# Start of an AdaLN/FFN kernel: up's second quarter on SP's queue, squares of group three behind x's first half, up's rest in two

## The reference

```python
w = weights[conditions]                       # (128, 32, 32) out of (200, 32, 32)
hs = einsum('bct,bcd->bdt', x, w)             # x: (128, 32, 256)
top = top_k(hs @ gate_w, 2)                   # 8 experts, only the two values are used
h = square(relu(hs @ up_w))                   # 256 -> 1024
y = h @ down_w + (hs @ expert_w) * top.sum()  # 1024 -> 256
out = x + (y - mean(y)) / sqrt(var(y) + 1e-5) * gamma + beta
```

## Time and profile before

| | us |
|---|---|
| median of 3 runs | 229.46 (229.46 to 229.64) |
| the profiled execution | 229.29 |
| its span, first to last instruction | 227.6 |
| TensorE busy | 220.9 (97% of the span) |
| VectorE busy | 160.9 (71%) |
| GpSimd busy | 131.4 (58%) |
| ScalarE busy | 106.4 (47%) |
| mean granted TensorE clock | 0.998 of full speed |

### The profile page before, as it was taken

One profiled execution on the slowest core, in us unless ns is written; L12 is line 12 of the kernel. 1 busy time (PEld: TensorE's weight loads), 2 busy tenths in 40 slices (PEclk: granted clock), 3 DMA queues, 4 the chain that ended last, 5 costly groups with the idle time before them and its releaser, 6 DMA issues.

```text
span 227.6 us, 3998 instructions
## 1 busy us (share of the span) xinstructions
PE 220.9 (97%) x1260; PEld 191.4 (84%) x1260; DVE 160.9 (71%) x352; ACT 106.4 (47%) x187; POOL 131.4 (58%) x131
## 2 busy tenths in 40 slices
PE   7899999999999999999999999999999999999992
PEld 2798888888888889888889888888888888888892
DVE  6587965777667777667667766577766766777885
ACT  3379865444555345534545444544454444444000
POOL 3758795665545763656455764366555575557411
PEclk9999999999999999999999999999999999999999
DMA  3877123030603010000200002000020002000031
GB/s 98 231 213 230 50 59 103 10 98 7 187 10 98 9 66 30 0 0 3 92 0 0 3 0 95 3 0 0 0 95 1 0 0 68 28 0 0 10 108 69
DMA packets 17177, 11.81 MB, mean 52 GB/s; under 512 B 6660, under 2 KB 16900, under 8 KB 17156
## 3 DMA queue, kind: packets, MB, share of 16 engines
q1 hardware_dynamic: 15460, 10.43, 15.1%
q10 hardware_dynamic: 1280, 1.07, 1.4%
q0 software_dynamic: 416, 0.05, 0.2%
HBM read 7.35 MB, written 4.19 MB: 51 GB/s over the span
## 4 chain that ended last, share of the span: by engine, by line
PE 94%; DMA 1%; issue 1%; DVE 1%; ACTq 1%; POOLq 0%; POOL 0%; ACT 0%; DVEq 0%
PE up_ps L337 39%; PE down_ps L431 25%; PE down_ps L433 13%; PE hid_ps L303 5%; PE moe_ps L449 3%; PE moe_ps L448 3%; PE moe_ps L447 3%; DMA wd<-in_L_cond_weights_dram 1%; PE down_ps L303 1%; ACTq L513 1%; DMA cond_row<-in_itok_B_dram 1%; POOLq L46 0%; POOL rstd L697 0%; DVE result L615 0%; DVE stats L588 0%
## 5 line engine op out<-in xcount | busy, mean ns | idle before, releaser
L682 POOL TENSOR_TENSOR sq_lo<-square,sq_hi 128x512 fp32r<-128x512 f32 x64 | 84.4, 1322 | 77.0 <-DVE square L553 77.0
L431 PE MATMUL down_ps<-down_hl,sq_hi 128*128 128x512 f32 x248 | 88.8, 393 | 0.0
L553 DVE SCALAR_TENSOR_TENSOR square<-up_ps,relu 128x512 f32<-128x512 f32 x64 | 44.0, 687 | 37.3 <-ACT relu L491 28.2
L433 PE MATMUL down_ps<-down_hl,sq_lo 128*128 128x256 f32 x248 | 69.6, 280 | 0.0
L431 PEld LDWEIGHTS down_ps<-down_hl,sq_hi 128*128 128x128 f32 x248 | 46.5, 188 | 10.8 <-issue 0.3
L491 ACT ACTIVATE relu<-up_ps 128x512 f32<-128x512 f32 x64 | 38.2, 596 | 35.8 <-PE up_ps L337 35.7
L337 PE MATMUL up_ps<-hid_hi,up_hi 128*128 128x512 f32 (+1 forms) x136 | 52.8, 391 | 0.3 <-ACT hid_hi L476 0.3
L337 PE MATMUL up_ps<-hid_hi,up_lo 128*128 128x512 f32 (+1 forms) x136 | 51.1, 379 | 0.0
L433 PEld LDWEIGHTS down_ps<-down_hl,sq_lo 128*128 128x128 f32 x248 | 46.7, 188 | 2.4
L493 ACT ACTIVATE sq_hi<-relu 128x512 fp32r<-128x512 f32 x64 | 40.6, 634 | 2.0
L337 PE MATMUL up_ps<-hid_lo,up_hi 128*128 128x512 f32 (+1 forms) x136 | 40.6, 381 | 0.0
(11 more groups left out here) (62 smaller groups left out, 193.3 us busy)
## 6 DMA issues: line engine op xcount, KB each, us to landing
x_sb<-in_x_dram SPq DMA_DIRECT2D x7, 512.0 KB, 4.2
out_dram<-result SPq DMA_DIRECT2D x7, 512.0 KB, 3.0
wd<-in_L_cond_weights_dram SPq DMA_DIRECT2D x111, 4.0 KB, 1.5
x_sb<-in_L_ffn_down_w_dram SPq DMA_DIRECT2D x2, 512.0 KB, 4.7
x_sb<-in_x_dram ACTq DMA_DIRECT2D x2, 256.0 KB, 2.9
result<-in_L_ffn_up_w_dram ACTq DMA_DIRECT2D x2, 256.0 KB, 2.9
result<-in_L_ffn_up_w_dram SPq DMA_DIRECT2D x1, 512.0 KB, 4.7
out_dram<-result SPq DMA_DIRECT2D x4, 128.0 KB, 1.7
```

Of the source, the lines that this page charges most:

```text
L431: pe.matmul(dst[:, :], a_hi, down_hl[:, c, :, :].rearrange("p s t -> p (s t)"), start=(c == 0), stop=False)
L433: mm = pe.matmul(dst[:, T:2 * T], a_lo, down_hl[:, c, 0, :], start=False, stop=(c == CH - 1))
L553: dve.scalar_tensor_tensor(square[:, c % 2, :], up_ps[c % UPB][:, :], 0.0, relu[:, c % 2, :], ALU.max, ALU.mult).then_inc(square_done, 1)
L682: pool.tensor_tensor(sq_lo[:, j % 2, c, :], square[:, c % 2, :], sq_hi[:, j % 2, c, :].bitcast(f32), ALU.subtract).then_inc(sq_lo_done, 1)
```

## The change

Four things move, all of them in the first 20 us of the program. The number and shape of the matmuls stay the same.

- Up's second quarter is issued by SP directly behind the first part of the condition row; before, ScalarE issued it behind the rounding of the first quarter. The rest of the condition row, before on SP, is the first thing that GpSimd issues.
- Of the squares of groups three and four, GpSimd issues 8 to 11 (the whole of group three) and waits for x's first half before it does; SP issues 12 to 15 (the whole of group four). TensorE waits for each group by a semaphore of its own, and the products of the second half run group by group.
- Up's second half is still one load (`UP_LOADS`), but it is rounded and split in two parts (`UP_SPLITS` has four now): chunks 4 and 5 where the whole was before, chunks 6 and 7 behind the experts' subtraction and behind the second square.
- ScalarE's queue has one load less, so x's second half is issued right behind the rounding.

```diff
-UP_SPLITS = [slice(0, 2), slice(2, 4), slice(4, CH)]
+UP_LOADS = [slice(0, 2), slice(2, 4), slice(4, CH)]
+UP_SPLITS = [slice(0, 2), slice(2, 4), slice(4, 6), slice(6, CH)]
...
-BY_SP, BY_ACT, BY_POOL, BY_SP_LATER = (0, 2, 4, 6), (1, 3, 5, 7), (8, 9, 10, 11, 12), (13, 14, 15)
+BY_SP, BY_ACT, BY_POOL, BY_SP_LATER = (0, 2, 4, 6), (1, 3, 5, 7), (8, 9, 10, 11), (12, 13, 14, 15)
...
-            cond_flat = cond.rearrange("(o b) -> o b", o=1)
             sp.dma_start(cond_row[:, 0:TILES * Q], cond_flat[:, 0:TILES * Q]).then_inc(cond_first_landed, 16)
-            sp.dma_start(cond_row[:, TILES * Q:ROWS_B], cond_flat[:, TILES * Q:ROWS_B]).then_inc(cond_later_landed, 16)
+            load_up(sp, 1)
             sp.wait_ge(cond_first_landed, 16)
...
             for b in BY_SP_LATER:
-                sp.dma_start(square_of(b), weights_of(values[b])).then_inc(wd_later_landed[0], 16)
+                sp.dma_start(square_of(b), weights_of(values[b])).then_inc(wd_first_landed[b // Q], 16)
...
             def conditioning_first(half):
                 pe.wait_ge(x_first_landed[half], 16)
-                if half == 0:
-                    pe.wait_ge(wd_first_landed[0], 16 * Q)
-                    condition(0, 0, 0)
-                    condition(0, 1, 0)
-                    pe.wait_ge(wd_first_landed[1], 16 * Q)
-                    condition(0, 0, 1).then_inc(hid_done, 1)
-                    condition(0, 1, 1).then_inc(hid_done, 1)
-                else:
-                    pe.wait_ge(wd_later_landed[0], 16 * len(BY_SP_LATER))
-                    pe.wait_ge(wd_later_landed[1], 16 * len(BY_POOL))
-                    for k in range(K):
-                        condition(0, k, 2)
-                        condition(0, k, 3).then_inc(hid_done, 1)
+                g = 2 * half
+                pe.wait_ge(wd_first_landed[g], 16 * Q)
+                condition(0, 0, g)
+                condition(0, 1, g)
+                pe.wait_ge(wd_first_landed[g + 1], 16 * Q)
+                condition(0, 0, g + 1).then_inc(hid_done, 1)
+                condition(0, 1, g + 1).then_inc(hid_done, 1)
...
             split_up(0)
-            load_up(act, 1)
             load_x_first(act, 1)
...
+            def round_up(part):
+                dve.tensor_copy(up_hi[:, :, split_cols(part)], up_raw[:, :, split_cols(part)]).then_inc(up_hi_ready, 1)
...
             dve.wait_ge(up_landed[2], 16)
-            dve.tensor_copy(up_hi[:, :, split_cols(2)], up_raw[:, :, split_cols(2)]).then_inc(up_hi_ready, 1)
+            round_up(2)
             split_up(2)
...
                             .then_inc(eg_lo_ready, 1)
+                        round_up(3)
+                    if j == 0 and c == 1:
+                        split_up(3)
...
+            pool.dma_start(cond_row[:, TILES * Q:ROWS_B], cond_flat[:, TILES * Q:ROWS_B]).then_inc(cond_later_landed, 16)
             pool.memset(minus_half[:, :], -0.5).then_inc(consts_ready, 1)
...
             pool.wait_ge(wd_zeroed[0], 1)
+
+            pool.wait_ge(x_first_landed[0], 16)
             for b in BY_POOL:
-                pool.dma_start(square_of(b), weights_of(values[b])).then_inc(wd_later_landed[1], 16)
+                pool.dma_start(square_of(b), weights_of(values[b])).then_inc(wd_first_landed[b // Q], 16)
```

More of the change, by code:

```diff
@@ L109, in adaln_ffn @@
         x_landed = {j: sem(f"x_landed{j}") for j in range(1, BLOCKS)}
-        up_landed = [sem(f"up_landed{n}") for n in range(len(UP_SPLITS))]
+        up_landed = [sem(f"up_landed{n}") for n in range(len(UP_LOADS))]
         down_landed = [sem(f"down_landed{n}") for n in range(DOWN_LOADS)]
@@ L113, in adaln_ffn @@
         cond_first_landed, cond_later_landed = map(sem, ("cond_first_landed", "cond_later_landed"))
-        wd_first_landed = [sem(f"wd_first_landed_group{g}") for g in range(TILES // 2)]
-        wd_later_landed = [sem("wd_later_landed_sp"), sem("wd_later_landed_pool")]
+        wd_first_landed = [sem(f"wd_first_landed_group{g}") for g in range(TILES)]
         wd_second_landed = [sem("wd_second_landed_sp"), sem("wd_second_landed_pool")]
@@ L220, in weights_of, with load_up @@
             return cond_w[bass.ds(row, 1), :, :].rearrange("s c d -> (s c) d")
-        def load_up(queue, part):
-            cols = split_cols(part)
-            queue.dma_start(up_raw[:, :, cols], up_rows[:, :, cols]).then_inc(up_landed[part], 16)
+        cond_flat = cond.rearrange("(o b) -> o b", o=1)
+        def load_up(queue, load):
+            cols = slice(P * UP_LOADS[load].start, P * UP_LOADS[load].stop)
+            queue.dma_start(up_raw[:, :, cols], up_rows[:, :, cols]).then_inc(up_landed[load], 16)
         def load_x_first(queue, half):
```

## The result

The changed kernel takes 230.51 us (median of 6 runs, 230.46 to 230.62) against 229.55 for the kernel before on the same chip (229.39 to 229.78). The ratio is 1.0041, 95% interval 1.0028 to 1.0054: 0.94 us slower. The forecast was 229.6 with a range up to 230.2, so the time lies outside it, on the slower side; "no change" had been given 0.66. Of the executions named further down, one of e10's twelve (277.2 us, at a granted clock of 0.757) is left out of its ratio.

A forecast was written before the change was run, and what follows sets the result against it. TensorE, with 94% of the chain of waits, was taken as the bound. From 229.29 us, +0.2 for the start and -0.07 for the split gave 229.42; with 0.17 to the median, 229.6, range 229.2 to 230.2.

The forecast's parts named there:

- part 5: Up's rest in two parts on VectorE: first chunk's square about 0.4 earlier, -0.07 us; second parts and later squares cost 0.
- The 0.07 behind chunk 3: TensorE's lateness at chunk 4, 14.48 instead of 14.41, waiting for the first square's bank; forecast to go, -0.07 us.
- Part 1: Up's second quarter on SP at the start: squares land later behind the larger bulk, +0.2 us, range -0.3 to +0.75.
- parts 1 to 4: Start +0.2 us; ScalarE's queue, groups three and four with GpSimd's wait, and SP's later issues each 0.
- Part 3: Groups three and four: GpSimd's squares wait for x's first half, starting about 4.5, landing 9.1, wanted 9.73; cost 0.
- Part 4: All of SP's later issues move by 0.5, second block's squares wanted at 16.69; cost 0, range 0 to +0.45 us.
- A: Crowded start: first two groups' squares pile up behind 768 KB, landing 0.5 to 0.75 later; 230.0 us; chance 0.18.
- B: Second block's squares: SP's 0.5 delay reaches TensorE at 16.69, +0.45, 229.9 us; chance 0.10.
- C: Freer start: with GpSimd silent, group two lands up to 0.3 earlier; 229.1 us; chance 0.10.
- D: GpSimd's issue is held: its squares miss 9.73 by 0.5 or more; 229.9 to 230.1 us; chance 0.04.
- the 0.26 for "slower": Chance of exceeding 229.92 us: A 0.15, half of B 0.05, D and a tail of the forecast 0.06.

The follow-up runs named there:

- e10: Kernel before with up's rest in two parts and the experts' rounding and subtraction ahead of the first relu and square; ratio 1.0012, 0.28 us over before.
- e2: Kernel before with up's rest rounded and split in two parts, loads unchanged; ratio 1.0037, 0.85 us over before.
- e1: Changed kernel with up's rest rounded and split whole, as before; ratio 1.0001 against the kernel before (0.9992 to 1.0009).
- e4: Changed kernel with GpSimd's first square rest waiting for the experts' subtraction; ratio 1.0027, 0.62 us over the kernel before.
- e6: Changed kernel with the experts' rounding and subtraction ahead of the first relu and square; ratio 0.9995 against the kernel before.
- e5: Changed kernel with both operations on up's last quarter moved behind the third square; ratio 1.0053, 1.2 us over the kernel before.
- e8: Kernel before with only GpSimd's squares held until x's first half has landed; ratio 1.0035, 0.8 us over before.
- e7: e3 with GpSimd's squares also held until x's first half has landed; ratio 1.0019, 0.44 us over the kernel before.
- e3: Kernel before with up's second quarter issued by SP, the row's rest behind it, GpSimd's squares not held; ratio 1.0039, 0.9 us over before.
- e9: e6 with squares 6 and 7 of the second group issued by GpSimd without the hold; ratio 1.0047, 1.1 us over the kernel before.
- e11: e10 with squares 6 and 7 issued by GpSimd and 11 to 15 by SP; ratio 1.0099, 2.3 us over the kernel before.

## Why the prediction was wrong, point by point

- **The step that failed is part 5**: "Cost 0" for the second parts, with "the squares of chunks 1 and 2 come some 0.4 later at most, with four banks ahead". The second square came 1.57 later, and the cost was 0.85 (e2) to 0.92 (after against e1). I had looked for the consumer of the squares among the banks `up_ps`, where there was indeed room. The consumer with little cover was another: GpSimd's chain of rests, and behind it the scale of the experts in VectorE's queue, with 0.39 to TensorE. It had its rows in the trace (GpSimd without a break from 14.48 to 21.62) and I did not follow them.
- The same part missed **what an earlier operation triggers**. "The square can start about 0.4 earlier" was right, but its only user in the next microsecond was GpSimd, which then worked beside the experts' subtraction. That the subtraction doubles by it (0.71 to 1.48) is shown by e4. That the order of this turn decides is shown by e6, where both added operations stay and the loss goes; behind a flipped turn the rounding makes the lateness larger (e5). The 0.07 behind chunk 3 did go away: chunk 4 follows at 0.24 after the last pair instead of 0.31.
- **Part 1 (start, +0.2)** was right in kind and in size as far as the runs can tell: 0.2 to 0.4 by e1, e5 and e6. The changed kernel's own profile has +0.47, but TensorE's slow warm-up bounds it there. ScalarE's squares landed in 2.2 to 2.6 instead of 1.7 to 2.0:

```profile
DMA to landing us min/median/max: 2.2/2.4/2.6
```

  The bulk was through between 4.5 and 5.0 (the slices have 378 and then 99 GB/s), as worked out. But the three loads did not end together, and x's first half was not later, as the prediction had it: it took 2.7 (2.8 in the kernel before) and landed at about 3.7, up's second quarter at 4.5 (3.2 after its issue) and up's first quarter at 5.3 (3.8, where before none of ScalarE's loads took more than 3.1). In the total the delay of the start was nearly given back: e1, which is parts 1 to 4 alone, is level with before within 0.2, where the parts' sum had been +0.2.
- **Part 3 (GpSimd's hold, cost 0)**: the cost is right for the changed kernel. GpSimd issued from 4.46, and TensorE's products at 10.19 did not wait. That the start met the 4.5 of the prediction is luck: x's first half landed earlier than assumed, at 3.7, and the 0.7 that GpSimd's queue needs from there to the issue was not in the sum. In the kernel before, the hold moves the squares as far (to 4.61) and costs 0.8 (e8). That the same lateness costs in one kernel and not in the other was not foreseen, and which of their differences makes it so is open.
- **Part 4 (SP's 0.5 later, cost 0)**: right. The landing times of these squares fell to as little as 2.7, and TensorE went from the experts' products to the second block's at 17.21 without a wait.
- **The rivals.** A was the reason given for a slower time, and half of it happened (the start) without costing. B, C and D did not happen. None of them was the flipped turn, so the 0.26 for "slower" stood on the wrong ground.

## What to carry to other kernels

When an operation is made earlier, list who is released by it and on which engine that one runs beside others; here the earlier square released GpSimd 0.36 before VectorE's next operation on SBUF instead of just behind it, and this turned a saving of 0.07 into a loss of 0.9. Follow a chain that has no break (GpSimd's five rests) to its last reader before calling an insertion on its feeder free; the cover is at that reader, not at the nearest buffer. And a part that is neutral in a bundle need not be so alone: the hold and the moved load cost 0.8 and 0.9 by themselves, 0.44 as a pair (e7), and nothing measurable together with the changed kernel's other queues (e1).

## What the runs showed of the hardware

- VectorE's operations that read only SBUF take longer beside a GpSimd `tensor_tensor`: the experts' subtraction (528 columns) took 0.71 alone and 1.48 to 1.82 when GpSimd had begun first; a 512-wide subtraction 0.69 and 1.65, a rounding 0.42 and 1.12 (e5). When VectorE began first (by 0.07 in e1), it took 0.71. The Trainium skill (SBUF — State Buffer, "Who interferes with whom") says that `tensor_tensor` with both inputs in SBUF contends with GpSimd's reads; the trace agrees (0.71 against 1.48 to 1.82). In all five executions in which GpSimd had begun first (after, e2, e3, e5, e7), the subtraction ended 0.55 to 0.58 behind the end of GpSimd's operation, whether it had started 0.04 or 0.37 behind its start. That is as if it did its work only when GpSimd was through, so what a flipped turn costs depends on how much of GpSimd's 1.29 is still ahead. VectorE's square, which reads one input from PSUM, stayed at 0.69 beside GpSimd.
- A square of 4 KB issued by GpSimd for the first block landed between 1.8 and 3.9 us after its issue, one for the second block in the kernel before in 4.0 to 4.6. The first two of e9 took 2.1 to 2.2, those of e11 3.0 to 3.6, with ScalarE's next two loads issued right behind them (4.54 and 4.98). What makes the difference was not settled.
- At the start TensorE runs at the lower of its two levels, and the moment of the rise differs from execution to execution: in the kernel before it falls within the ten warm-up products (3.87 for all, end at 5.5), in e2 the first group's products at 6.01 are still slow (0.77 instead of 0.46). It moved the start by 0.65 at the same loads (7.74 and 8.39), while the records show a granted clock of 1.00 in both. A single profile of before and one of after do not tell a start's change of a few tenths.
